# One head's order of steps rewritten on four engines of an attention kernel, with the score masks of every head written by ScalarE, and five edits ahead of the loop

## The chip, the cores and the metric

One NeuronCore of a Trainium2 chip runs the whole program in one launch. Its engines work side by side, each through its own list in order: TensorE (PE in the profile, its weight loads PEld), VectorE (DVE), ScalarE (ACT), GpSimd (POOL) and SyncE (SP), which only issues DMAs. Engines wait for each other through counting semaphores. The metric is device time in microseconds; lower is better.

## What is computed

x has 8 sequences of 128 tokens and 512 features. A LoRA-adapted linear layer makes h. Attention over h has 32 query heads, 8 key and value heads, head size 128, int4 weights with a scale per 128 inputs, rotary position and a causal mask. A LoRA pair and a feed-forward part with int8-rounded weights and activations follow.

```python
    x = x + _L0_attn_ref(_L0_cond_ref(x, itok_B_0_23, L0_cond_W, L0_cond_b, L0_cond_lora_As, L0_cond_lora_Bs), ...)
    x = x + _L0_ffn_ref(_L0_cond2_ref(x, L0_cond2_A, L0_cond2_B, itok_B_4_50), ...)
...
        q = _dequant_matmul(hidden_states, qw_q, scales_q).reshape(b, s, NH, HD).transpose(0, 2, 1, 3)
        q = _apply_rope(q, cos, sin)
        k = _apply_rope(k, cos, sin)
        scores = jnp.einsum('bhqd,bhkd->bhqk', q, k) / math.sqrt(HD)
        scores = jnp.where(causal[None, None], scores, jnp.finfo(scores.dtype).min)
        attn = jax.nn.softmax(scores.astype(jnp.float32), axis=-1).astype(q.dtype)
        ctx = jnp.einsum('bhqk,bhkd->bhqd', attn, v)
        return _dequant_matmul(ctx, qw_o, scales_o)
```

## The kernel before

**Stages.** x and W are turned, h is made in two halves (f = 0 and 1, four sequences each) and split into an upper and a lower fp16 part (h_hi, h_lo). Then comes the loop over 8 groups g (one key and value head each) with 4 query heads h in each; group 0 and group 7 are written out (`first`, `last`), groups 1 to 6 are a hardware loop. Then the second LoRA pair and the feed-forward part.

**Steps.** A step (`double_step`) is four fp16 matmuls of 128x512 into one of three PSUM pairs (pair0 to pair2, two banks each). `(Q, j)`, `(K, j)` and `(V, j)` project input block j of the next head's query or of the next group's key or value; the partial results must be scaled by block, so each step is drained on its own: block 0 by ScalarE (`drain_first`), blocks 1 to 3 by VectorE (`drain`), into raw_q, raw_k, raw_v. `(O, c)` multiplies the context by the output weights for output block c; VectorE adds it to accT (`add_output`), except block 3 of three heads in four, which ScalarE scales to part_out (`part_output`) and an accumulating DMA of POOL adds. The list PERIOD sets the order of steps, and `pair_of` which pair a step takes (its place in the list modulo 3), so a step may start when the step three places before it is drained (`free_pair`).

**One head beside the steps.** In the two banks flow0 and flow1, one for each half f, come in turn: scores (matmul of queries and keys), their row maxima (`maxima`, VectorE), the exponentials (`exps`, ScalarE), the row sums' reciprocals (`inverse`, VectorE), the multiplication by them (`normalise`: half 0 on POOL, half 1 on ScalarE), the turned probabilities (`turn_probs`, PE; kept in probsT by ScalarE, `keep_turned`), the context (`context`, PE), and its split in ctx_hi (ScalarE, `keep_upper_context`) and ctx_lo (VectorE, `split_context`). The causal mask reaches a score bank in one of two ways: PE adds it by a matmul with the identity (`scores` with masked false), or ScalarE writes it first (`seed_mask`) and the scores are accumulated onto it. Before, ScalarE does this for the heads 0 to 2 of a group and PE at head 3 (`SEEDED`).

**Other engines.** POOL does rotary position: a cosine and a sine product and a sum for each half (`q_cosine`, `q_sine`, `q_add`; for keys at heads 2 and 3). The sine product needs swap_q, raw_q with its halves of partitions exchanged, by a DMA of SP that is issued when (Q, 3) is drained. SP also loads the integer weights (`load_q`, `load_kv`, `load_output`); ScalarE makes them fp16 (`dequant`). At the end of a group PE turns the values of the next in two parts (`values_ahead`), through flow0 and flow1, and ScalarE keeps them in v_now.

**Ahead of the loop** the same is done for the first key, value and the first two queries in smaller pieces (`early_project`, `early_wide`, `early_groups`), in between the making of h. `lora_round(f, s)` adds the LoRA part to h by 32-row matmuls, in four rounds of which each waits for the one before; `linear(k)` is one output block of the dense part.

## Time and profile before

| | us |
|---|---|
| median of 3 runs | 559.31 |
| the runs | 554.47, 559.31, 561.33 |
| the profiled execution | 560.78 |
| its span, first to last instruction | 558.7 |

| engine | busy us | share |
|---|---|---|
| PE | 534.9 | 96% |
| PEld | 332.7 | 60% |
| DVE | 477.6 | 85% |
| ACT | 429.0 | 77% |
| POOL | 383.3 | 69% |

The page gives busy time by engine, the span in 40 slices, the DMA queues, the chain of work that ended last (82% of it PE, 8% DVE) and the costliest groups of instructions. A matmul's own time (0.38 us for 512 columns) overlaps the next one's, so what a matmul costs is the distance from its start to the next start. PEclk is the clock that PE was granted, 1 being 2.4 GHz and 0.5 being 1.2 GHz. In the order-of-time view a row has start, length, engine, source line and what is written from what; in square brackets stands the idle time ahead of it and what ended it. "PE flow L1702" is the context, L1694 the turned probabilities, L1567 the scores, L1564 the mask matmul, L1578 and L1579 the steps, L841 `keep_turned`, L1265 `add_output`, L1249 `drain`.

### The profile page before, as it was taken

The page shows a single profiled execution, that of the slowest core. Times are in us where ns is not written, and L with a number is a line of the kernel's source. Part 1 is how long each engine was busy: PE and PEld are TensorE (multiplying, and loading weights), DVE is VectorE, ACT ScalarE, POOL GpSimd, SP SyncE. Part 2 cuts the span into 40 slices and gives each one's busy share as a digit, 9 for nine tenths or more (in the row PEclk, how much of TensorE's full clock was granted, in tenths as well). Part 3 has the DMA queues.
Part 4 walks back from the last instruction along what each step waited for, and adds up shares of the span by engine and source line. Part 5 has one row for each costly group of instructions (what it writes and reads, how often), then busy time and mean ns, then how long its engine had stood idle before and what let it go on. Part 6 is the DMA issues. An engine that isn't in the chain of part 4 may idle for free.

```text
span 558.7 us, 10860 instructions
## 1 busy us (share of the span) xinstructions
PE 534.9 (96%) x3190; PEld 332.7 (60%) x3190; DVE 477.6 (85%) x629; ACT 429.0 (77%) x1091; POOL 383.3 (69%) x400
## 2 busy tenths in 40 slices
PE   8999979999999999999999999999999999987985
PEld 6744456666666666666666666666666666653442
DVE  4885957999899899989998999899989998876897
ACT  3574558878888888788878887888788878876795
POOL 3005485799779877987799779867986897741063
PEclk9989999999999999999999999999999999999899
DMA  8931344742673267327733672367336532410003
GB/s 295 271 74 38 82 107 133 170 95 57 170 178 88 57 177 175 79 66 177 176 69 75 176 181 61 82 177 168 70 82 169 131 79 72 96 38 1 1 20 132
DMA packets 41341, 63.47 MB, mean 114 GB/s; under 512 B 12452, under 2 KB 20804, under 8 KB 41316
## 3 DMA queue, kind: packets, MB, share of 16 engines
q1 hardware_dynamic: 35652, 46.94, 32.3%
q0 software_dynamic: 3648, 12.75, 11.3%
q10 hardware_dynamic: 2016, 3.48, 2.0%
q8 instruction: 12, 0.20, 0.1%
q14 instruction: 13, 0.11, 0.1%
HBM read 28.55 MB, written 2.10 MB: 55 GB/s over the span
## 4 chain that ended last, share of the span: by engine, by line
PE 82%; DVE 8%; ACT 4%; issue 2%; DMA 2%; POOL 1%; ACTq 0%; SPq 0%; DVEq 0%; POOLq 0%
PE pair L1578 22%; PE pair L1579 22%; PE flow L1702 11%; PE flow L1567 9%; PE flow L1694 6%; PE pair L1485 3%; PE pair L1507 1%; DVE y_max L1361 1%; DMA swap_q<-raw_q 1%; PE flow L1572 1%; DVE accT L1265 1%; ACT probs L779 1%; PE flow L1485 1%; DVE probs L1373 1%; DVE rope_c L1373 1%
## 5 line engine op out<-in xcount | busy, mean ns | idle before, releaser
L1265 DVE SCALAR_TENSOR_TENSOR accT<-pair,so_now,accT 128x1024 f32<-128x1024 f32 x103 | 130.9, 1277 | 19.8 <-PE pair L1579 16.2
L1249 DVE SCALAR_TENSOR_TENSOR raw_q<-pair,sc_now,raw_q 128x1024 f32<-128x1024 f32 x90 | 115.4, 1282 | 7.0 <-ACT raw_q L835 3.9
L572 POOL TENSOR_TENSOR rope_s<-swap_q,consts 128x512 f32<-128x512 f32 x62 | 85.4, 1378 | 30.6 <-DMA swap_q<-raw_q 30.6
L1578 PE MATMUL pair<-ctx_hi,wo 128*128 128x512 f16 x256 | 97.0, 379 | 4.2 <-issue 2.3
L1579 PE MATMUL pair<-ctx_lo,wo 128*128 128x512 f16 x256 | 97.0, 379 | 0.0
L1578 PE MATMUL pair<-h_hi,wq 128*128 128x512 f16 x240 | 91.0, 379 | 0.2 <-ACT raw_q L835 0.2
L779 ACT ACTIVATE probs<-flow,negmax 128x128 f32<-128x128 f32 x248 | 87.3, 368 | 4.9 <-DVE negmax L1217 4.9
L1579 PE MATMUL pair<-h_lo,wq 128*128 128x512 f16 x240 | 91.0, 379 | 0.0
L584 POOL TENSOR_TENSOR qT<-rope_c,rope_s 128x512 f32<-128x512 f32 x62 | 85.5, 1379 | 4.6
L572 POOL TENSOR_TENSOR rope_c<-raw_q,consts 128x512 f32<-128x512 f32 x62 | 77.6, 1274 | 10.7 <-DVE raw_q L1249 10.3
L1702 PEld LDWEIGHTS flow<-probsT,v_now 128*128 128x128 f32 x512 | 62.9, 193 | 19.2 <-ACT probsT L841 15.3
L1702 PE MATMUL flow<-probsT,v_now 128*128 128x128 f32 x512 | 72.3, 286 | 2.1 <-ACT probsT L841 2.0
L1567 PEld LDWEIGHTS flow<-kT,qT 128*128 128x128 f32 x496 | 65.1, 192 | 7.1 <-ACT flow L859 0.2
L1567 PE MATMUL flow<-kT,qT 128*128 128x128 f32 x496 | 65.4, 275 | 0.0
L864 ACT ACTIVATE ctx_hi<-flow,ctx_gain 128x512 f16<-128x512 f32 x64 | 43.9, 687 | 27.8 <-PE flow L1702 25.5
L610 POOL TENSOR_TENSOR probs<-probs,rowinv 128x512 f32<-128x512 f32 x32 | 33.3, 1040 | 37.3 <-DVE rowinv L1236 37.3
L1272 DVE SCALAR_TENSOR_TENSOR ctx_lo<-flow,ctx_gain,ctx_hi 128x512 f16<-128x512 f32 x64 | 47.5, 744 | 10.7 <-ACT ctx_hi L864 10.2
L779 ACT ACTIVATION_READ_ACCUMULATOR probs<-flow,negmax 128x1 f32 x248 | 51.6, 208 | 0.0
L841 ACT ACTIVATE probsT<-flow 128x512 f32<-128x512 f32 x64 | 38.2, 596 | 8.2 <-PE flow L1694 8.2
L1578 PEld LDWEIGHTS pair<-ctx_hi,wo 128*128 128x128 f16 x256 | 25.1, 98 | 31.2 <-issue 4.1
L835 ACT ACTIVATE raw_q<-pair,sc_now 128x1024 f32<-128x1024 f32 x30 | 33.4, 1114 | 13.2 <-PE pair L1579 11.6
L1578 PE MATMUL pair<-h_hi,wkv 128*128 128x512 f16 x112 | 42.8, 383 | 0.0
(281 smaller groups left out, 1008.5 us busy)
## 6 DMA issues: line engine op xcount, KB each, us to landing
swap_q<-raw_q SPq DMA_DIRECT2D x62, 256.0 KB, 3.7
accT<-part_out POOLq DMA_DIRECT2D x22, 512.0 KB, 4.5
wq_i<-in_L_attn_qw_q SPq DMA_DIRECT2D x8, 1024.0 KB, 5.6
wo_i<-in_L_attn_qw_o SPq DMA_DIRECT2D x32, 256.0 KB, 2.8
swap_k<-raw_k SPq DMA_DIRECT2D x14, 256.0 KB, 3.6
wkv_i<-in_L_attn_qw_k SPq DMA_DIRECT2D x8, 256.0 KB, 3.7
wkv_i<-in_L_attn_qw_v SPq DMA_DIRECT2D x8, 256.0 KB, 4.1
stage<-in_x ACTq DMA_DIRECT2D x4, 256.0 KB, 4.7
```

Of the source, the lines that this page charges most:

```text
L572: pool.tensor_tensor(per_seq(into[:, f, :]), per_seq(source[:, f, :]), on_each_seq(table), ALU.mult).then_inc(done, 1)
L584: pool.tensor_tensor(qT[:, (h + 1) % 2, half[f]], rope_c[:, f, :], rope_s[:, f, :], ALU.add).then_inc(q_roped, 1)
L779: e = act.activation(probs[:, 0, f, seq(b)], bank[:, seq(b)], ACT.Exp, bias=negmax[:, f, b:b + 1], accum_out=rowsum[:, f, b:b + 1])
L841: act.activation(probsT[:, f, :], flow[f][:, :], ACT.Copy).then_inc(probsT_kept, 1)
L864: act.activation(ctx_hi[:, h % 2, half[f]], flow[f][:, :], ACT.Copy, scale=ctx_gain[:, 0:1]).then_inc(ctx_kept, 1)
L1249: dve.scalar_tensor_tensor(out=into, in0=flat(pair[pair_of(h, (kind, j), last, first)][:, :, :]), scalar=sc_now[:, scale_slot(kind, h), j: ...
L1265: dve.scalar_tensor_tensor(out=a, in0=flat(pair[pair_of(h, (O, c), last, first)][:, :, :]), scalar=so_now[:, (h if c == 0 else h - 1) % 2, ...
L1272: dve.scalar_tensor_tensor(out=ctx_lo[:, h % 2, half[f]], in0=flow[f][:, :], scalar=ctx_gain[:, 0:1], in1=ctx_hi[:, h % 2, half[f]], op0=A ...
L1567: mm = pe.matmul(bank[:, seq(b)], qT[:, par, t], kT[:, t], start=False, stop=(b == HB - 1), skip_group_check=masked)
L1578: pe.matmul(into[:, f, :], w, upper[:, half[f]], start=True, stop=False)
L1579: mm = pe.matmul(into[:, f, :], w, lower[:, half[f]], start=False, stop=True)
L1702: mm = pe.matmul(flow[f][:, seq(b)], v_now[:, HB * f + b, :], probsT[:, f, seq(b)], start=(b == 0), stop=(b == HB - 1), skip_group_check=True)
```

## The change

**In the loop.** PE turns the probabilities of half 0 after (Q, 1), not after (Q, 2), so two steps stand between them and the first context; a step then stands between the first context and the second turning. At head 2, (V, 1) moves behind (O, 2). ScalarE writes the mask for head 3's successor too, so no mask matmul is left in the groups' heads. The values of the next group are turned as a step of its own, (VALUES, 0), through a PSUM pair, and kept by ScalarE with one instruction of 1024 elements. ScalarE's list is written anew (below). VectorE takes the reciprocals for half 0 directly behind (O, 0) of the head before, ahead of the maxima for half 1, and those for half 1 behind (Q, 1). POOL normalises half 0 at head 0 ahead of the sine product. SP swaps before it loads output weights, and at head 1 loads query, key and value weights first. Heads 0 and 1 of the last group take the new order too; its heads 2 and 3 keep the old.

**Ahead of it.** SP issues the first full swap of raw_q ahead of the four loads for the feed-forward part, and the load of the second key and value weights ahead of two half swaps. The first step (Q, 0) stands in front of turning the first values; VectorE, not ScalarE, keeps these; the first head's (K, 1) moves ahead of its second context. ScalarE makes h_hi of one block (`HI_BY_ACT`) itself. A quarter of the first chunk of `linear(4)` stands behind each LoRA round, and only the other three chunks remain behind them.

The core of the diff:

```diff
         PERIOD = [[(Q, 0), (O, 1), (Q, 1), (Q, 2), (Q, 3), (K, 0), (O, 2), (O, 3), (K, 1), (O, 0)],
                   [(Q, 0), (O, 1), (Q, 1), (Q, 2), (Q, 3), (K, 2), (O, 2), (O, 3), (K, 3), (O, 0)],
-                  [(Q, 0), (O, 1), (Q, 1), (Q, 2), (Q, 3), (V, 0), (V, 1), (O, 2), (O, 3), (V, 2), (O, 0)],
-                  [(Q, 0), (O, 1), (Q, 1), (Q, 2), (V, 3), (Q, 3), (O, 2), (O, 3), (O, 0)]]
+                  [(Q, 0), (O, 1), (Q, 1), (Q, 2), (Q, 3), (V, 0), (O, 2), (V, 1), (O, 3), (V, 2), (O, 0)],
+                  [(Q, 0), (O, 1), (Q, 1), (Q, 2), (V, 3), (Q, 3), (O, 2), (VALUES, 0), (O, 3), (O, 0)]]
         STEPS = [(h, s) for h in range(REP) for s in PERIOD[h]]
         SKIPPED = 3
         ADDED_BY_DMA = (O, 3)
...
-            return h < SEEDED and not (last and h >= 2)
+            return not (last and h >= 2)
...
+        HI_BY_ACT = C + 1
...
+            load_kv(1)
...
+                if k == HI_BY_ACT:
+                    act.activation(h_hi[:, c, half[f]], linear_bank(k), ACT.Identity, bias=bias_gained[:, c:c + 1],
+                                   scale=gain[:, 0:1]).then_inc(hi_by_act, 1)
...
+            dequant_kv(1, 0)
             act.wait_ge(outputs_in_unit, 1)
-            for f in range(2):
-                act.wait_ge(vT_done, f + 1)
-                act.activation(v_now[:, HB * f:HB * f + HB, :], per_seq(banks[4 + f]), ACT.Copy).then_inc(v_kept, 1)
...
+                    def keep_values():
+
+                        act.wait_ge(step_done, steps_by(g, h, (VALUES, 0), first, last))
+                        act.activation(v_flat, flat(pair[pair_of(h, (VALUES, 0))][:, :, :]), ACT.Copy).then_inc(act_drained, 1)
...
                     if not (first and h == 0):
                         exps(n, 0, score_bank(0, last and h == 3))
-                        if present(h, (Q, 0), first, last):
-                            drain_query()
+                    if h < 2 and not last and not (first and h == 0):
+                        dequant_kv(g + 1, h)
+                    if present(h, (Q, 0), first, last):
+                        drain_query()
                     exps(n, 1, score_bank(1, last and h == 3))
-                    if h < 2 and not last:
-                        dequant_kv(g + 1, h)
-                    if last:
+                    if last and h >= 2:
                         normalise(1)
                     keep_turned(0)
-                    if not last:
+                    if not (last and h >= 2):
                         normalise(1)
-                    if last:
+                        keep_upper_context(0)
+                        keep_turned(1)
+                    else:
                         keep_turned(1)
                         keep_upper_context(0)
-                    else:
-                        keep_upper_context(0)
-                        keep_turned(1)
-                    if first and h == 0:
-                        seed_mask(0)
                     if h == 0 and not last:
                         act.wait_ge(k_scale_set, g + 1)
                         act.wait_ge(k_roped, 2 * g + 2)
@@ -918,13 +913,15 @@
                     if h == 2 and not last:
                         act.wait_ge(v_scale_set, g + 1)
                         drain_first(V, g + 1)
+                    seed_mask(0)
                     keep_upper_context(1)
+                    output_weights()
                     if h == 3 and not last:
-                        keep_values(g + 1, 0)
-                    if not (first and h == 0):
-                        seed_mask(0)
+                        keep_values()
+                    part_output()
                     seed_mask(1)
-                    part_output()
+                    if h < REP - 1 and present(h + 1, (Q, 0), False, last) or h == REP - 1 and not last:
+                        dequant_q(g + (h + 3) // REP, (h + 3) % REP)
...
-                    inverse(0)
+                    if first and h == 0:
+                        inverse(n, 0)
+                        for f in range(2):
+                            keep_values(f)
+                        inverse(n, 1)
                     add_output(1)
-                    if not (first and h == 0):
-                        inverse(1)
                     if last and h >= 2:
+                        inverse(n, 1)
                         add_output(2)
                         add_output(3)
                     for j in range(1, C):
                         drain(*((V, 3) if h == 3 and j == 3 else (Q, j)))
-                        if first and h == 0 and j == 1:
-                            inverse(1)
+                        if j == 1 and not (last and h >= 2) and not (first and h == 0):
+                            inverse(n, 1)
                     split_context(0)
                     if h == 1:
                         drain(K, 2)
+                    if h == 3:
+                        drain(Q, 3)
+                    if not (last and h >= 2):
+                        add_output(2)
                     if h == 2:
                         drain(V, 1)
-                    if h == 3:
-                        drain(Q, 3)
                     split_context(1)
                     if not (last and h >= 2):
-                        add_output(2)
                         add_output(3)
...
+                    if not (last and h == 3):
+                        inverse(n + 1, 0)
...
+            def linear_piece(k, b):
+
+                pe.matmul(linear_bank(k)[:, seq(b)], WT[:, 0, seq(k - C)], accT[:, 0, seq(HB + b)], start=(b == 0), stop=False,
+                          skip_group_check=True)
+
             pe.wait_ge(u_kept, 1)
             for s in range(HB):
                 lora_round(0, s)
+                linear_piece(4, s)
 
...
-            linear(4)
+            for c in range(1, C):
+                linear_chunk(4, c)
...
+                    if first and h == 0:
+                        pe.wait_ge(early_added, 18)
+                        for f in range(2):
+                            turn_values(f, banks[4 + f])
+                        pe.wait_ge(lowT_kept, 2)
...
+                    project(Q, 1)
+                    turn_probs(0)
+                    project(Q, 2)
+                    project(*((V, 3) if h == 3 else (Q, 3)))
+                    context(0)
+                    project(*((K, 0), (K, 2), (V, 0), (Q, 3))[h])
+                    turn_probs(1)
+                    output(2)
                     if h == 2:
-                        project(V, 0)
                         project(V, 1)
+                    if first and h == 0:
+                        project(K, 1)
+                    context(1)
                     if h == 3:
-                        project(Q, 3)
-                    context(1)
-                    if not (last and h >= 2):
-                        output(2)
-                    values_ahead(0)
-                    if not (last and h >= 2):
-                        output(3)
+                        values_ahead()
+                    output(3)
```

The order of PE's instructions at three places. REGISTER_ALU and ISA rows are waits on a loop-dependent count.

**PE, head 0 of a group in the loop, from behind the turning of half 0 (flow0<-consts,probs) on.** Before, one step, (Q, 3) into pair1, stands in front of the context, and the turning of half 1 behind it:

```order
L1660 REGISTER_ALU
L1578 MATMUL pair1<-h_hi,wq 128x512
L1579 MATMUL pair1<-h_lo,wq 128x512
L1578 MATMUL pair1<-h_hi,wq 128x512
L1579 MATMUL pair1<-h_lo,wq 128x512
L1699 ISA
L1700 ISA
L1702 MATMUL flow0<-probsT,v_now 128x128 x4
L1694 MATMUL flow1<-consts,probs 128x128 x4
```

After, two steps, (Q, 2) into pair0 and (Q, 3) into pair1:

```order
L1596 MATMUL pair0<-h_hi,wq 128x512
L1597 MATMUL pair0<-h_lo,wq 128x512
L1596 MATMUL pair0<-h_hi,wq 128x512
L1597 MATMUL pair0<-h_lo,wq 128x512
L1675 REGISTER_ALU
L1596 MATMUL pair1<-h_hi,wq 128x512
L1597 MATMUL pair1<-h_lo,wq 128x512
L1596 MATMUL pair1<-h_hi,wq 128x512
L1597 MATMUL pair1<-h_lo,wq 128x512
L1716 REGISTER_ALU
L1717 ISA
L1719 MATMUL flow0<-probsT,v_now 128x128 x4
```

One step more now separates the turning from the context, and the turning of half 1 no longer follows the context.

**PE, head 3 of a group, behind the second context.** Before, (O, 2) has been issued, the values' first half is turned through flow0, then (O, 3), then the mask (tri_b) and the scores:

```order
L1710 REGISTER_ALU
L1572 MATMUL flow0<-consts,raw_v 128x128 x4
L1578 MATMUL pair2<-ctx_hi,wo 128x512
L1579 MATMUL pair2<-ctx_lo,wo 128x512
L1578 MATMUL pair2<-ctx_hi,wo 128x512
L1579 MATMUL pair2<-ctx_lo,wo 128x512
L1719 REGISTER_ALU
L1725 REGISTER_ALU
L1564 MATMUL flow0<-tri_b,ident_b 128x512
L1567 MATMUL flow0<-kT,qT 128x128 x4
```

After, the values are one step of eight turned blocks into pair2, and no mask matmul is left:

```order
L1719 MATMUL flow1<-probsT,v_now 128x128 x4
L1725 REGISTER_ALU
L1730 MATMUL pair2<-consts,raw_v 128x128 x8
L1675 REGISTER_ALU
L1596 MATMUL pair0<-ctx_hi,wo 128x512
L1597 MATMUL pair0<-ctx_lo,wo 128x512
L1596 MATMUL pair0<-ctx_hi,wo 128x512
L1597 MATMUL pair0<-ctx_lo,wo 128x512
L1738 ISA
L1742 REGISTER_ALU
L1743 REGISTER_ALU
L1585 MATMUL flow0<-kT,qT 128x128 x4
```

The values left the flow banks, and what was two mask matmuls on PE is now two instructions of ScalarE.

**ACT, the end of head 3 and the loop's edge.** Before (v_now<-flow keeps the values, wo and wq are weights made fp16, probs the exponentials):

```order
L864 ACTIVATE ctx_hi<-flow0,ctx_gain 128x512
L841 ACTIVATE probsT<-flow1 128x512
L864 ACTIVATE ctx_hi<-flow1,ctx_gain 128x512
L851 ISA
L852 ACTIVATE v_now<-flow0 128x512
L362 REGISTER_ALU
L362 COMPARE_AND_BRANCH
L754 ACTIVATE wo<-wo_i 128x512
L754 ACTIVATE wq<-wq_i 128x512
L852 ACTIVATE v_now<-flow1 128x512
L779 ACTIVATE probs,rowsum<-flow0,negmax 128x128 x4
```

After (flow0<-consts and flow1<-consts write the mask):

```order
L842 ACTIVATE probsT<-flow1 128x512
L860 ACTIVATE flow0<-consts 128x512
L865 ACTIVATE ctx_hi<-flow1,ctx_gain 128x512
L757 ACTIVATE wo<-wo_i 128x512
L852 REGISTER_ALU
L853 ACTIVATE v_now<-pair2 128x1024
L860 ACTIVATE flow1<-consts 128x512
L757 ACTIVATE wq<-wq_i 128x512
L361 REGISTER_ALU
L361 COMPARE_AND_BRANCH
L782 ACTIVATE probs,rowsum<-flow0,negmax 128x128 x4
```

The weights moved from a head's start to its end, and the mask of the first half now stands ahead of the second ctx_hi. The same order holds at heads 0 to 2.

## Rows read from the trace of the kernel before

**Rows 1.** The page's first line: the span of the profiled execution.

```profile
span 558.7 us, 10860 instructions
```

**Rows 2.** Busy time in stretches: from:to, length, engines, PEclk, DMA share, GB/s.

```profile
33.50:37.00 3.50, 3.50 (x12) 1.51 (x5) 3.36 (x10) 3.29 (x6) 0.43 (x3) 0.51 0.17 23
...
81.10:85.00 3.90, 3.88 (x16) 3.08 (x17) 2.30 (x3) 2.81 (x7) 3.50 (x5) 0.56 0.33 63
99.80:155.00 55.20, 55.18 (x333) 35.33 (x333) 49.84 (x57) 45.55 (x123) 45.50 (x48) 1.00 0.51 125
```

**Rows 3.** PE in the loop, in order of time: start us, us, what [idle before].

```profile
166.38 1.05 PE L1702 MATMUL flow<-probsT,v_now 128*128 128x128 f32 x8
167.27 0.38 PE L1578 MATMUL pair<-ctx_hi,wo 128*128 128x512 f16 x1
...
182.69 0.38 PE L1579 MATMUL pair<-ctx_lo,wo 128*128 128x512 f16 x1
182.97 0.39 PE L1564 MATMUL flow<-tri_b,ident_b 128*128 128x512 bf16 x1
183.19 1.05 PE L1567 MATMUL flow<-kT,qT 128*128 128x128 f32 x8
...
190.01 0.60 PE L1694 MATMUL flow<-consts,probs 128*128 128x128 f32 x4
190.45 0.38 PE L1578 MATMUL pair<-h_hi,wq 128*128 128x512 f16 x1
...
191.31 1.15 PE L1702 MATMUL flow<-probsT,v_now 128*128 128x128 f32 x8
192.46 0.66 PE L1694 MATMUL flow<-consts,probs 128*128 128x128 f32 x4
192.96 0.38 PE L1578 MATMUL pair<-h_hi,wkv 128*128 128x512 f16 x1
```

**Rows 4.** Waits, whole span: engine line <- releaser: us, times, longest.

```profile
PEld flow L1702 <- ACT probsT L841: 15.3, 48, 0.3
```

**Rows 5.** Order of time: DVE, POOL, PE at one head, ACT at another.

```profile
173.43 0.68 DVE L1217 TENSOR_REDUCE negmax<-flow 128x4 f32<-128x512 f32 x1
...
174.27 1.04 POOL L610 TENSOR_TENSOR probs<-probs,rowinv 128x512 f32<-128x512 f32 x1 [0.79 <-DVE rowinv L1236]
...
175.96 0.60 PE L1694 MATMUL flow<-consts,probs 128*128 128x128 f32 x4
...
190.65 0.60 ACT L841 ACTIVATE probsT<-flow 128x512 f32<-128x512 f32 x1
```

**Rows 6.** Groups of DVE in 99.8 to 155.0 us: busy, mean ns, idle.

```profile
L1265 DVE SCALAR_TENSOR_TENSOR accT<-pair,so_now,accT 128x1024 f32<-128x1024 f32 x14 | 17.8, 1278 | 1.8 <-PE pair L1579 1.8
L1249 DVE SCALAR_TENSOR_TENSOR raw_q<-pair,sc_now,raw_q 128x1024 f32<-128x1024 f32 x12 | 15.4, 1280 | 0.5
```

**Rows 7.** Order of time, first head of the first group: PE, SP's queue, ACT.

```profile
73.66 1.09 PE L1572 MATMUL pair<-consts,raw_v 128*128 128x128 f32 x8 [0.85 <-DVE raw_v L1210]
...
78.11 0.39 PE L1578 MATMUL pair<-h_hi,wq 128*128 128x512 f16 x1 [0.23 <-ACT raw_q L835]
...
81.12 1.85 PE L1702 MATMUL flow<-probsT,v_now 128*128 128x128 f32 x8 [1.97 <-ACT probsT L841]
...
69.89 1.11 SPq L464 DMA_DIRECT2D swap_q<-raw_q  x2
...
76.94 1.11 ACT L835 ACTIVATE raw_q<-pair,sc_now 128x1024 f32<-128x1024 f32 x1 [1.45 <-DMA swap_q<-raw_q]
```

**Rows 8.** Order of time, ahead of the loop: PE, then DVE.

```profile
31.80 0.50 PE L1498 MATMUL pair<-raw_v,qT 32*128 32x128 f32 x8 [0.17 <-PE pair L1498]
...
54.28 2.30 DVE L1148 CAST h_hi<-h_scaled 128x512 f16<-128x512 f32 x2 [2.44 <-ACT h_scaled L730]
```

**Rows 9.** Order of time, first head of the last group: PE.

```profile
468.11 0.66 PE L1694 MATMUL flow<-consts,probs 128*128 128x128 f32 x4 [0.32 <-ACT probs L846]
...
473.55 0.38 PE L1578 MATMUL pair<-ctx_hi,wo 128*128 128x512 f16 x1 [0.23 <-DVE accT L1265]
```

More of the change, by code:

```diff
@@ L264, in present @@
                 return False
-            return not (last and (s[0] in (K, V) or s[0] == Q and h >= 2))
+            return not (last and (s[0] in (K, V, VALUES) or s[0] == Q and h >= 2))
         def added_by_dma(h, s, last):
@@ L494, in body @@
                         swap(swap_k, raw_k, swapped_k)
+                    if h < 2 or not last:
+                        load_output(g + h // 2, (h + 2) % REP)
             body(0, True, False)
@@ L1704, in context, with values_ahead @@
                         mm.then_inc(pv_done, 1)
[L1706 to L1712 removed]
+                    def values_ahead():
+                        pe.wait_ge(dve_drained, drains_by(g, h, (V, 3), first, last))
+                        free_pair(VALUES, 0)
+                        into = pair[pair_of(h, (VALUES, 0))]
+                        for f in range(2):
+                            for b in range(HB):
+                                mm = pe.transpose(into[:, f, seq(b)], raw_v[:, f, seq(b)], ident)
+                        mm.then_inc(step_done, 1)
                     def scores_ahead(f):
@@ L1728, in body @@
                     project(Q, 0)
-                    output(1)
-                    project(Q, 1)
-                    project(Q, 2)
-                    if not last:
-                        turn_probs(0)
-                    project(*((V, 3) if h == 3 else (Q, 3)))
+                    if first and h == 0:
+                        pe.wait_ge(early_added, 18)
+                        for f in range(2):
+                            turn_values(f, banks[4 + f])
+                        pe.wait_ge(lowT_kept, 2)
+                    output(1)
                     if last and h >= 2:
```

106 lines of the change are left out of this document (41 added, 65 removed).

## The prediction

> **What bounds the kernel now.** The page comes first: the span is 558.7 us [rows 1], and the time of that execution, 560.78, lies 2.1 above it. I sum against 560.8; the median of the runs, 559.31, is 1.5 lower. The chain that ended last is four fifths PE, and the stretch view says where that holds: in 99.8 to 155.0 us, one group of four heads, PE is busy in 55.18 of 55.20 us at clock 1.00, VectorE in 49.84, ScalarE in 45.55, POOL in 45.50 [rows 2]. So in the loop PE alone sets the pace, and "busy" hides what it could save. The order-of-time view shows it as start-to-start distances. A step is 0.86 (190.45 to 191.31), a turning 0.44 (190.01 to 190.45). A context costs 0.89 where two steps stand ahead of it (166.38 to 167.27), but 1.15 with one step (191.31 to 192.46), and the turning behind that one takes 0.50 instead of 0.44 (192.46 to 192.96) [rows 3]. The waits name the cause: the context's weight loads waited 48 times for ScalarE's copy L841, 15.3 us [rows 4]. A mask matmul costs 0.28: it starts 0.28 behind the matmul ahead of it, of which 0.22 is that one's own length, and itself holds PE for 0.22 (182.69, 182.97, 183.19) [rows 3], so the two mask matmuls at a group's edge are 2 x (0.06 + 0.22) = 0.56.
>
> **The loop, part by part.**
> The first context. ScalarE's copy starts at 190.65 and takes 0.60 [rows 5], so it ends at 191.25 and PE starts at 191.31. With (Q, 2) moved behind the turning, PE asks 0.86 later. The copy is then 0.8 us early, and the context costs 0.89. The turning of half 1 follows a step and costs 0.44. Gain 0.26 + 0.06 = 0.32 a head. It holds for 27 heads: 32 without the first and without the last group's four. 27 x 0.32 = 8.6 us. The second context still has one step in front and I credit it nothing.
> The weight load itself may be priced another way. The Trainium skill (TensorE: Matmul & The Clock Gate, LDWEIGHTS) estimates a load of 128 columns at 128/1.2 = 107 ns. If only such a load were exposed, the term would be 27 x 0.11 = 2.9 us, and the sum 546.2. The measured distances, 1.15 against 0.89, are of the same instructions and decide.
> The masks. Seven group edges times 0.56 = 3.9 us off PE. ScalarE pays two more masks, bounded by its copies of the same 512 elements, 0.60 each [rows 5], and saves one instruction of the two that kept the values. Its load becomes about 45.55 + 1.2 = 46.8 a group.
> The values turn in one step of eight blocks instead of two of four: the same 0.88. It adds a stop: (O, 0) of head 3 takes pair2 behind it and needs ScalarE's copy.
> The new period is 55.2 - 4 x 0.32 - 0.56 = 53.4 us. Does anyone else fit no longer? VectorE has 49.84 of work in it (93%), ScalarE 46.8 (88%), POOL 45.5 (85%). VectorE's instructions are the same ones, 14 and 12 of its two largest groups, of 1.28 us [rows 6]; only the order moves. So I look at waits, not loads.
> The tightest is the turning of half 0. POOL normalises at 174.27 for 1.04, ends at 175.31, and PE turns at 175.96, spare 0.65 [rows 5]. The turning moves 0.86 forward, which would leave it 0.21 late; but VectorE now takes the reciprocal ahead of a maximum of 0.68 (173.43) [rows 5], so about 0.4 to spare is left. At head 0 POOL no longer has a sine product in front. Following each engine's new list over one head with the durations above, I find 0.2 to 0.4 us spare for the first context, the second half's mask and (O, 0) of head 3. All are positive and all are thin. I take no loss; the bounds are nothing and 0.3 a head, which is giving back the gain.
> SP: the weight loads now go ahead of head 1's swap. What they wait for (weights made at the end of head 0 and early in head 1) is done some 6 us before (Q, 3) is drained, so the swap isn't held; cost nothing.
>
> **The first head.** Before it, PE waits 0.85 for the last piece of V, 0.23 for ScalarE's drain, and 1.97 for the first context's copy [rows 7]. Then it runs at clock 0.56 for 3.9 us, which costs 3.9 x 0.44 = 1.7 [rows 2]. The reason is a queue: the swap is issued at 69.89 behind four loads, ScalarE's drain starts only at 76.94, released by it [rows 7], and everything of the head stands behind that drain. With the loads behind the swap I expect the drain near 74, where POOL's cosine products end. (Q, 0) fills the 0.85. ScalarE has no values to keep and no output weights in between. So 0.85 + 0.23 + 1.97 + 1.7 = 4.75 goes. What comes: the mask of half 0 now stands behind the key's drain, and the split of half 1 ends late for (O, 0); I put 0.5, between 0 and 1.1. Net 4.3.
>
> **Ahead of the loop.** LoRA rounds have 0.17 us of idle each [rows 8]; the quarter chunks (0.22 each) fit there, so one chunk, 0.88, goes. Right behind, PE runs at clock 0.51 for 3.5 us, costing 1.7 [rows 2]; denser rounds may or may not prevent that, and from ends equally far I take half, 0.9. For h_hi, VectorE's two casts take 2.30 us together [rows 8] on the path to the second half's projections; with one of them on ScalarE's side I count 0.65 (bounds 0 and 1.5).
>
> **The last group.** Heads 0 and 1 wait 0.32 before the second turning and 0.23 before (O, 0) [rows 9] and have no K step to space things. The new order removes some and keeps some: 0.5 a head, 1.0 in all (0 to 1.6).
>
> **Sum.** 8.6 + 3.9 + 4.3 + 0.9 + 0.9 + 0.65 + 1.0 = 20.25. 560.8 - 20.25 = 540.5 us. 2%, about what a measurement of this kernel can tell from no change, is 11.2 us, so faster begins at 548.1.
>
> **Rivals.**
> A, the forecast: 535 to 546, chance 0.70. Both ends of the clock and the first head's bounds lie in it.
> B, only a weight load's worth comes back at the first context (2.9 for 8.6): 546.2. For it: the second context with one step ahead still loses some. Against it: 0.89 at 166.38 with two steps [rows 3]. Chance 0.07.
> C, ScalarE comes late. Its list is full of waits, and the thin margins turn into 0.3 us a head at the first context or the mask. 31 x 0.3 = 9.3, so 549.8. For it: ScalarE goes from 45.55 of 55.2 to 46.8 of 53.4. Against: it idles between, and what it does late is now the weights, which nobody wants soon. Chance 0.10.
> D, the other sign: VectorE stands still at the new place of the first reciprocal. There it waits for the exponentials of the next head, and behind it are the maxima of half 1 and (O, 1)'s drain, for whose pair PE waits. Each us that the exponentials are late is then a us of PE in each of 31 heads. It decides at 20.25 / 31 = 0.65 us; at 1.0 us the time is 571. For it: VectorE has only 7% left. Against: by my walk the exponentials end at about the time (O, 0) is drained. Chance 0.06.
> E, still faster than 535: both low-clock stretches gone and the second context's wait too. Chance 0.07.
> The change not doing what it says would be B.
>
> **Numbers.** Faster: A, B, E, 0.84 in all, of which I give 0.01 to same; the chances are 0.83, 0.12, 0.05, D being partly within 2%. Range 535 to 549: all of A and B and the near part of C.
>
> **What would show it.** In the changed kernel's order-of-time view the first context's distance should be 0.89 and no mask matmul should stand at group edges; a group should take 53.4 us. PE idle ahead of the first context of all should be under 0.3, and ScalarE's first drain should start near 74 (less what was won before). Wrong would be: weight loads of the context still waiting for the copy (B, C), PE waiting for VectorE's drains or reciprocal waits growing (D), or PE waiting for the mask or ctx_lo.

## The result, and the profile after

The median is 540.57 us (538.78 to 543.61, 4 runs) against 558.54 (554.47 to 561.33, 4 runs): a ratio of 0.9698, 95% interval 0.9652 to 0.9744. Run again later with 6 runs, the changed kernel took 539.84 against 557.57, a ratio of 0.9681 (0.9648 to 0.9713). The profiled execution took 543.61, its span is 541.1.

The page of the changed kernel, its first lines:

```profile
span 541.1 us, 10845 instructions
...
PE 520.7 (96%) x3182; PEld 333.6 (62%) x3182; DVE 475.0 (88%) x630; ACT 428.6 (79%) x1097; POOL 383.6 (71%) x400
```

Its busy time in three stretches (from:to, length, PE, PEld, DVE, ACT, POOL, PEclk, DMA share, GB/s), which answer to [rows 2]: at the end of the LoRA rounds and behind them, around the first context, and one group of the loop:

```profile
33.50:37.00 3.50, 3.50 (x25) 2.08 (x26) 3.33 (x11) 2.19 (x4) 0.43 (x3) 1.00 0.15 19
76.00:80.00 4.00, 4.00 (x26) 2.64 (x25) 3.79 (x5) 3.23 (x8) 3.58 (x5) 1.00 0.00 0
183.22:236.64 53.42, 53.42 (x329) 35.54 (x328) 49.41 (x56) 45.53 (x125) 45.38 (x48) 1.00 0.52 128
```

A group takes 53.42 us instead of 55.26, TensorE is still the one that is always busy, and both low-clock stretches of [rows 2] are at full clock. One head of the loop on TensorE, in order of time, beside [rows 3] (L1719 is the context, L1709 the turning, L1596 and L1597 the steps):

```profile
236.64 1.05 PE L1719 MATMUL flow<-probsT,v_now 128*128 128x128 f32 x8
237.53 0.38 PE L1596 MATMUL pair<-h_hi,wkv 128*128 128x512 f16 x1
...
238.40 0.60 PE L1709 MATMUL flow<-consts,probs 128*128 128x128 f32 x4
238.83 0.38 PE L1596 MATMUL pair<-ctx_hi,wo 128*128 128x512 f16 x1
...
239.69 1.15 PE L1719 MATMUL flow<-probsT,v_now 128*128 128x128 f32 x8
240.68 0.38 PE L1596 MATMUL pair<-ctx_hi,wo 128*128 128x512 f16 x1
```

The first context costs 0.89 (236.64 to 237.53), the turning 0.43, the second context, with one step ahead, 0.99.

Where the time went, by marks on TensorE that both kernels have. The column "predicted" divides the prediction's own terms over the same stretches:

| from the mark ahead to | before | after | gained | predicted |
|---|---|---|---|---|
| first LoRA round | 31.13 | 31.68 | -0.55 | 0 |
| first projection | 42.21 | 41.00 | 1.76 | 1.8 |
| second scores | 71.75 | 70.53 | 0.01 | 0.65 |
| (Q, 0) of head 1, group 0 | 89.66 | 84.50 | 3.94 | 4.3 |
| (Q, 0) of head 0, group 1 | 131.30 | 124.77 | 1.37 | 1.52 |
| (Q, 0) of head 0, group 7 | 462.87 | 445.60 | 10.74 | 11.04 |
| first matmul behind the loop | 510.51 | 493.17 | 0.07 | 1.0 |

Behind that another 0.2 to 0.3 is gained, so the spans differ by 17.6. Where the programs are the same, these distances are the same within a few hundredths in all the runs below, but for four places: what comes ahead of the first LoRA round (28.8 to 31.7), one or two of the six groups (0.1 to 0.3 longer, up to 1.4 in three runs; most of it is explained behind run 7), the last group, and the feed-forward part. In this profile it is the first of the six groups, 53.69 instead of 53.42.

### The profile page after: what moved, and what is told of

Read it like the earlier page. It is cut to its first block, busy times and chain, and to the rows that moved or that the text cites. A ratio compares the mean times of both kernels' runs of the same rounds, so it can differ in the third digit from the quotient of the medians.

```text
span 541.1 us, 10845 instructions
## 1 busy us (share of the span) xinstructions
PE 520.7 (96%) x3182; PEld 333.6 (62%) x3182; DVE 475.0 (88%) x630; ACT 428.6 (79%) x1097; POOL 383.6 (71%) x400
## 4 chain that ended last, share of the span: by engine, by line
PE 82%; DVE 9%; ACT 4%; issue 2%; DMA 2%; POOL 1%; ACTq 0%; SPq 0%; DVEq 0%; POOLq 0%
PE pair L1596 22%; PE pair L1597 22%; PE flow L1719 10%; PE flow L1585 10%; PE flow L1709 5%; PE pair L1497 2%; DVE raw_q L1255 2%; PE pair L1519 2%; PE flow L1497 1%; PE pair L1730 1%; DVE y_max L1373 1%; DVE probs L1385 1%; ACT probs L782 1%; DVE rope_c L1385 1%; DMA stage<-in_x 1%
## 5 line engine op out<-in xcount | busy, mean ns | idle before, releaser
L1596 PE MATMUL pair<-ctx_hi,wo 128*128 128x512 f16 x256 | 97.0, 379 | 4.2 <-ACT wo L757 1.6
L1597 PE MATMUL pair<-ctx_lo,wo 128*128 128x512 f16 x256 | 97.0, 379 | 0.0
L1596 PE MATMUL pair<-h_hi,wq 128*128 128x512 f16 x240 | 91.0, 379 | 0.0
L1597 PE MATMUL pair<-h_lo,wq 128*128 128x512 f16 x240 | 91.0, 379 | 0.0
L1719 PEld LDWEIGHTS flow<-probsT,v_now 128*128 128x128 f32 x512 | 64.8, 191 | 13.3 <-ACT probsT L842 7.0
L1719 PE MATMUL flow<-probsT,v_now 128*128 128x128 f32 x512 | 69.5, 279 | 0.1
L782 ACT ACTIVATION_READ_ACCUMULATOR probs<-flow,negmax 128x1 f32 x248 | 53.3, 215 | 0.0
L842 ACT ACTIVATE probsT<-flow 128x512 f32<-128x512 f32 x64 | 38.9, 608 | 17.6 <-PE flow L1709 17.6
L847 ACT ACTIVATE probs<-probs,rowinv 128x128 f32<-128x128 f32 x128 | 40.9, 391 | 13.3 <-DVE rowinv L1242 12.6
L1219 DVE TENSOR_REDUCE negmax<-flow 128x4 f32<-128x512 f32 x62 | 42.0, 677 | 3.2 <-PE flow L1585 2.5
L1596 PE MATMUL pair<-h_hi,wkv 128*128 128x512 f16 x112 | 42.5, 379 | 0.0
```

The source lines that it names most:

```text
L782: e = act.activation(probs[:, 0, f, seq(b)], bank[:, seq(b)], ACT.Exp, bias=negmax[:, f, b:b + 1], accum_out=rowsum[:, f, b:b + 1])
L1219: dve.tensor_reduce(negmax[:, f, :], per_seq(score_bank(f, last_head)), AX.X, ALU.max, negate=True).then_inc(negmax_done, 1)
L1596: pe.matmul(into[:, f, :], w, upper[:, half[f]], start=True, stop=False)
L1597: mm = pe.matmul(into[:, f, :], w, lower[:, half[f]], start=False, stop=True)
L1719: mm = pe.matmul(flow[f][:, seq(b)], v_now[:, HB * f + b, :], probsT[:, f, seq(b)], start=(b == 0), stop=(b == HB - 1), skip_group_check=True)
```

## Experiments

Eleven runs are edits of the changed kernel, one is the changed kernel again. Runs 1, 3, 4 and 5 were on one chip, the others on another. The ratios are to the kernel before; to compare with, the changed kernel itself took 539.84 us (run 11), and run 5, on the first of the two chips, 539.79 with an edit that changed nothing. The intervals of the times are about as wide as most of these effects, so each reading below rests on distances in one trace. "From the first LoRA round" leaves out the part ahead that varies.

**1. The turning put back.**

```diff
                     project(Q, 1)
-                    turn_probs(0)
                     project(Q, 2)
+                    turn_probs(0)
```

> The changed kernel with one thing put back: TensorE turns the probabilities of half 0 behind (Q, 2), so only one step stands between them and the first context. Theory (the first context pays whatever part of its weight loads waits for ScalarE's copy): its distance goes from 0.89 back to 1.15, the turning of half 1 stays at 0.44, so 0.26 a head and 1.04 a group, 53.43 to 54.47; over 30 heads 7.8 us. Rival B (only a weight load of 0.11 is exposed): 0.44 a group, 53.87, 3.3 us in all. Rival D (VectorE or POOL set the pace, not TensorE): the group stays at 53.4.

Measured: 543.25 us, ratio 0.9764 (0.9727 to 0.9800). Five of the six groups took 53.86 to 53.88, one 54.06: 0.45 a group in the five, of which 0.36 are the first contexts. TensorE in it:

```profile
142.52 1.15 PE L1719 MATMUL flow<-probsT,v_now 128*128 128x128 f32 x8
143.50 0.38 PE L1596 MATMUL pair<-h_hi,wkv 128*128 128x512 f16 x1
```

With one step ahead the context costs 0.98, not 1.15. That is rival B's price, and the reading of [rows 3] on which the largest term rests was wrong: 0.26 was not what ScalarE's copy cost. (By the formula of the Trainium skill, TensorE: Matmul & The Clock Gate, LDWEIGHTS, a load of 128 columns is estimated at 107 ns. The 0.09 that the late copy exposes lies near it, but the profile gives 191 ns for a weight load of the context, so that it is one such load is not shown.) What else ended the 1.15 stood in a row that I had not read, ScalarE in the kernel before at the same head:

```profile
191.15 1.26 ACT L846 ACTIVATE probs<-probs,rowinv 128x128 f32<-128x128 f32 x4
```

It ends at 192.41, and TensorE turns half 1 at 192.46. So the turning may have waited for the normalised half, or it costs more directly behind a context.

The kernel before also had the price of a context with one step ahead and a step behind, at the same head. It is the second context:

```profile
193.82 1.15 PE L1702 MATMUL flow<-probsT,v_now 128*128 128x128 f32 x8
194.80 0.38 PE L1578 MATMUL pair<-ctx_hi,wo 128*128 128x512 f16 x1
```

That is 0.98 too. The 0.89 of [rows 3] (166.38) was a second context as well, with a step behind it, and the 1.15 a first one with the turning behind it: the two differ in what follows, not only in the steps ahead.

**2. The turning directly behind the context**, which tells these apart.

```diff
                     context(0)
-                    project(*((K, 0), (K, 2), (V, 0), (Q, 3))[h])
                     turn_probs(1)
+                    project(*((K, 0), (K, 2), (V, 0), (Q, 3))[h])
```

> The changed kernel with the turning of half 1 directly behind the first context again, the step that stood between them behind it; two steps still stand ahead of the context. What it tells apart: why the first context cost 1.15 before, of which turn_late gave back only 0.09 a head. Theory 1 (the turning waits for ScalarE's normalised probabilities, which end 1.14 behind the first context's start in the changed kernel): 1.19 to the turning and 0.50 for it, 0.36 a head, the group 53.42 to 54.87. Theory 2 (the turning's own weight loads can't go under the context's short matmuls): 1.06 and 0.50, 0.23 a head, 54.35. The prediction's step (only the number of steps ahead of the context counts): 0.06 a head, 53.67.

Measured: 547.87 us, ratio 0.9843 (0.9768 to 0.9919), a group 54.59. TensorE at one head:

```profile
237.44 1.05 PE L1719 MATMUL flow<-probsT,v_now 128*128 128x128 f32 x8
238.65 0.66 PE L1709 MATMUL flow<-consts,probs 128*128 128x128 f32 x4
239.14 0.38 PE L1596 MATMUL pair<-h_hi,wkv 128*128 128x512 f16 x1
```

1.21 and 0.49, as theory 1 has it, and ScalarE's multiplication of half 1 starts at 237.31 and takes 1.28, so it ends 0.06 ahead of the turning. Its group is 0.28 shorter than I wrote, because the step that moved now stands ahead of the second context, which costs 0.89 instead of 0.98 at three heads; 4 x 0.36 - 3 x 0.09 = 1.17, and 53.42 + 1.17 = 54.59. The turning waits for ScalarE. So the 0.32 a head are 0.09 for the copy, 0.17 for the normalised half, and 0.06 for a turning that starts from a wait. They don't come one by one: context and turning together take 1.70 in this run and took 1.65 before, so two steps ahead alone bring nothing. The step behind the context brings 0.23 (run 1 has it), and only then are the 0.09 of the copy to be had.

**3. The masks on TensorE at head 3 again** (seven pairs of mask matmuls; ScalarE doesn't write these).

```diff
-            return not (last and h >= 2)
+            return h < REP - 1 and not (last and h >= 2)
...
```

> The changed kernel with the masks of the heads that follow head 3 added by TensorE again, two mask matmuls at each of seven group edges, and ScalarE without them. Theory (TensorE sets the pace and each mask matmul costs its distance): 0.43 to 0.56 a group, 53.43 to between 53.86 and 53.99, 3.0 to 3.9 us in all. Rival C (ScalarE is late for something): the 1.04 us of ScalarE that go give part of it back, less than 0.4 a group.

Measured: 544.30 us, ratio 0.9782 (0.9752 to 0.9811), a group 53.86. That is 2 x 0.22, the matmuls alone. The 0.13 that is missing to my 0.56 was there in the kernel before, where a mask started 0.28 behind its neighbour, but doesn't come back with the mask. Which of the edits at the group's edge took it away, no run shows. Nothing of it is given back by ScalarE.

**4. The LoRA rounds side by side again.**

```diff
                 lora_round(0, s)
-                linear_piece(4, s)
...
-            for c in range(1, C):
-                linear_chunk(4, c)
+            linear(4)
```

> The changed kernel with the four LoRA rounds next to each other again and the whole first chunk of linear(4) behind them. From the changed kernel's trace, where the stretch from the first round to the first projection took 9.32 us against 11.08 before: if the clock falls to half again behind the rounds, 1.76 us come back and the filled idle time was worth nothing (theory: what the spacing brought was the clock, and the pieces cost as much as they filled). The prediction's own step says 0.88 for the chunk, with the clock apart: 0.9 if the clock stays, 2.6 if it falls. If the clock's fall had another cause, and the pieces cost what they fill: 0.

Measured: 541.70 us, ratio 0.9730 (0.9697 to 0.9762). From the first LoRA round to the first projection 11.06 us, against 9.32: 1.74. A stretch behind the rounds in this run, then TensorE's rows of it, then those of the changed kernel:

```profile
33.00:34.00 1.00, 1.00 (x9) 0.51 (x3) 1.00 (x1) 0.64 (x1) 0.43 (x3) 0.50 0.32 33
```

```profile
32.65 0.65 PE L1510 MATMUL pair<-raw_v,qT 32*128 32x128 f32 x8 [0.17 <-PE pair L1510]
33.23 8.64 PE L1497 MATMUL pair<-accT,WT 128*128 128x512 f32 x16
```

```profile
34.23 0.50 PE L1510 MATMUL pair<-raw_v,qT 32*128 32x128 f32 x8
34.67 0.49 PE L1556 MATMUL pair<-accT,WT 128*128 128x128 f32 x2
34.99 6.17 PE L1497 MATMUL pair<-accT,WT 128*128 128x512 f32 x14
```

The clock falls to 0.50 for some 3.5 us again, half of which is the 1.74. The filled idle time brought nothing: a round alone took 0.67 with its 0.17 of idle [rows 8], a round and a piece take 0.85 (0.44 from 34.23 to 34.67 are the round's). So a piece has TensorE for 0.42 (the last, with the long chunks behind it, for 0.32), not for the 0.22 of its columns. From the first round to the linear part it is 3.31 (31.68 to 34.99) against 2.43 (31.13 to 33.56) before, 0.88 more, exactly the chunk that went. Further on this run loses more than the 1.74: its first context is 2.29 later (47.07 from the first LoRA round, against 44.78), since other waits come up, one of 0.63 for ScalarE ahead of the second scores. How these hang on the 1.74 was not followed.

**5. Four loads ahead of the swap, and 6. all six.** In the first the four loads of the feed-forward part stand ahead of the first full swap again; in the second `load_kv(1)` too, SyncE's order of before.

```diff
+            load_kv(1)
+            for m, row in enumerate((gamma, beta, b1)):
+                sp.dma_start(rows[:, m, :], row.partition_broadcast(P)).then_inc(d_rows, 16)
+            sp.dma_start(b3_col[:, :], b3.rearrange("(c p) -> p c", p=P)).then_inc(d_rows, 16)
             sp.wait_ge(early_sin, 4)
             sp.wait_ge(early_added, 15)
             swap(swap_q, raw_q, swapped_q)
```

> The changed kernel with SyncE's four loads for the feed-forward part ahead of the first full swap again. Theory (the swap behind these loads held ScalarE's first drain): the drain, now at 73.3, starts near 75.7 (76.9 before, less 1.2 won ahead of it); the first context comes 2.0 to 2.4 later, TensorE idles there, and if the clock falls in the narrow stretch another 1.6 goes: 2.0 to 4.0 us in all. Rival (the drain waits for POOL's cosine products, not for the swap): less than 0.3.

> The changed kernel with all six loads (second key and value weights, the four of the feed-forward part) between the last half swap and the first full swap, SyncE's order of before. With only the four of them there nothing was lost, since the swap waited for POOL's sine product anyway. Theory (the transfer of the swap is slow behind the transfers of the six loads: 7.0 us from issue to ScalarE's drain before, 4.5 to 4.6 in the changed kernel and with four loads): 7 us again, the drain and the first context 2.2 to 2.4 later, and up to 1.7 more if TensorE's clock falls there; 2.2 to 4.0 us on the first context, counted from the first LoRA round (44.8 us in the changed kernel). Rival (the drain's place in ScalarE's own list, not the transfer, was what mattered): less than 0.3.

Measured with four: 539.79 us, ratio 0.9701 (0.9664 to 0.9738), first context 44.79 us from the first LoRA round against 44.78. My expectation fell. SyncE and POOL in that run:

```profile
64.88 0.43 SPq L473 DMA_DIRECT2D b_col<-in_L_ffn_b  x1
...
66.03 1.28 POOL L531 TENSOR_TENSOR rope_s<-swap_q,consts 128x512 f32<-128x512 f32 x1
```

The loads are issued long before POOL's sine product ends at 67.31, for which the swap must wait, and the swap goes out at 67.34. In the kernel before it was the same: the sine product ended at 69.85, the swap was issued at 69.89 [rows 7]. It never stood in a queue.

Measured with six: 542.44 us, ratio 0.9746 (0.9691 to 0.9800). The swap is issued at the same place (66.20, 36.99 us from the first LoRA round in both), but ScalarE starts 7.35 us later instead of 4.62:

```profile
73.55 1.11 ACT L836 ACTIVATE raw_q<-pair,sc_now 128x1024 f32<-128x1024 f32 x1 [4.39 <-DMA swap_q<-raw_q]
...
74.72 0.39 PE L1596 MATMUL pair<-h_hi,wq 128*128 128x512 f16 x1 [1.43 <-ACT raw_q L836]
76.69 1.61 PE L1719 MATMUL flow<-probsT,v_now 128*128 128x128 f32 x8 [0.94 <-ACT probsT L842]
```

Its stretch behind that:

```profile
78.00:80.00 2.00, 2.00 (x7) 0.91 (x7) 1.90 (x2) 0.69 (x1) 1.00 (x3) 0.50 0.00 0
```

The first context is 2.70 later, TensorE idles 2.37 and its clock falls to 0.50 behind that; at head 1 4.1 us are lost, all that the first head had gained. What held the drain was the transfer, slow while the data of six loads issued just ahead of it still moved. Whether it is their number, their shape or their time was not tried: with six the last load was issued 1.3 us ahead of the swap, with four 2.5.

**7. The values turned first and kept by ScalarE**, with SyncE's new order.

> The changed kernel with the first values turned ahead of (Q, 0) and kept by ScalarE again, SyncE's new order left as it is. Theory, from the changed kernel's trace: TensorE waits 0.95 for the values before it turns them, and ScalarE's two copies stand ahead of its drain; the first context comes 0.9 to 1.3 later (44.8 to between 45.7 and 46.1, counted from the first LoRA round). Rival (since putting the six loads back alone cost 4.1 us at head 1, which is the whole gain of the first head, these two edits bring nothing): less than 0.3.

Measured: 541.75 us, ratio 0.9711 (0.9660 to 0.9762); the first context 46.09 against 44.8, so 1.3 us. These edits are worth 1.3 once the swap is fast, and the two parts overlap: 4.1 and 1.3 are more than the 3.94 gained.

This trace also has something that I overlooked, and that the edit has nothing to do with. The first of the six groups takes 54.83 instead of 53.42. ScalarE in it, then TensorE:

```profile
148.22 1.11 ACT L879 ACTIVATE part_out<-pair,so_now 128x1024 f32<-128x1024 f32 x1 [1.64 <-DMA accT<-part_out]
...
149.96 1.15 PE L1586 MATMUL flow<-kT,qT 128*128 128x128 f32 x8 [1.14 <-ACT flow L863]
```

ScalarE must wait for the accumulating DMA before it writes part_out anew, and since the change the mask of half 1 stands behind that instruction. When the transfer is late, TensorE waits for the mask. The same wait is 0.51 in the first profile of the changed kernel (its group is 0.27 longer), 0.89 in those of runs 2 and 3 (0.65 longer), 0.24 in run 4's (nothing), and the kernel before has none. That is of rival C's kind, at one or two heads of an execution.

**8. h_hi of the one block by VectorE again.**

> The changed kernel with h_hi of that one block made by VectorE again. The prediction's step says 0.65 us (0 to 1.5) on the path to the projections of the second half. From the changed kernel's trace: the second half's projections came 0.44 us nearer, but a projection of the first half waited 0.25 for VectorE and lay 0.5 later. Theory (the edit does nothing measurable in sum): within 0.3 us at the second scores, counted from the first LoRA round (38.85 us in the changed kernel). The prediction's step: 0.65 more, 39.5.

Measured: 539.66 us, ratio 0.9674 (0.9623 to 0.9725). The second scores lie 38.90 us from the first LoRA round, against 38.85: 0.05. The edit does nothing.

**9. The reciprocal behind the maxima again, and 10. one more instruction on ScalarE.**

```diff
-                    if not (last and h == 3):
-                        inverse(n + 1, 0)
                     if not (last and h >= 2):
                         maxima(n + 1, 1)
+                    if not (last and h == 3):
+                        inverse(n + 1, 0)
```

```diff
                     part_output()
+                    wait(act, extra_done, n)
+                    act.activation(per_seq(probs[:, 1, 0, :]), on_each_seq(tri), ACT.Copy).then_inc(extra_done, 1)
                     seed_mask(1)
```

> The changed kernel with VectorE's reciprocal for half 0 behind the maxima of half 1 again. Theory (it stands in front because the turning of half 0 has only 0.38 us to spare, 0.17 at head 3): the reciprocal comes 0.60 later, POOL's product with it, TensorE waits about 0.2 at each turning, 0.6 to 0.9 a group, 53.42 to between 54.0 and 54.3, 5 us in all. Rival D of the prediction (standing at the reciprocal costs VectorE, and TensorE with it): the group gets shorter than 53.4, by up to 0.4, which VectorE waits there at head 3.

> The changed kernel with one more instruction of 512 elements on ScalarE in every head, ahead of the mask of half 1; it writes a place that nobody reads. It takes 0.52 from its neighbours. Theory (spare from the changed kernel's trace: the mask ends 0.41, 0.39, 0.58 and 0.69 ahead of the scores at heads 0 to 3): heads 0 and 1 lose 0.11 and 0.13, the others nothing, the group 53.42 to about 53.7. Rival C of the prediction (ScalarE is at its end once the masks are its): 0.3 to 0.52 a head, 54.6 to 55.5.

Measured, reciprocal: 547.39 us, ratio 0.9835 (0.9773 to 0.9896), a group 54.50, 1.07 more. Its waits, from 180 to 450 us:

```profile
PEld flow L1709 <- POOL probs L610: 10.8, 20, 0.6
```

In the changed kernel this row reads 1.3 us in 6 times, the longest 0.2. A delay of 0.60 costs 0.27 a head, more than the 0.6 to 0.9 a group that I had expected, so the spare is about 0.33; rival D's mechanism isn't there, on the contrary.

Measured, ScalarE: 545.94 us, ratio 0.9809 (0.9737 to 0.9877), a group 54.18, 0.76 more or 0.19 a head for 0.52 put in, again a spare of 0.33. TensorE now waits ahead of the scores of half 1 at every head, where I had expected it at two:

```profile
PEld flow L1588 <- issue: 8.3, 20, 0.6
```

The row names no releaser; at the head where I looked the mask ended at 189.18 and the scores started at 189.31. Neither my 0.25 a group nor rival C's 1.2 to 2.1 came. ScalarE isn't at its end, but a third of a microsecond is all it has.

**11. The changed kernel again, and 12. a version with both ends reordered.** In the last group VectorE takes (O, 3) of head 2 behind the splits and maxima, and TensorE head 3's (O, 3) behind the contexts. In the first head the split of the first context and its mask go ahead.

```diff
                         context(0)
                         context(1)
+                        if h == 3:
+                            output(3)
...
                     if last and h == 2:
                         maxima(n + 1, 1, True)
+                        add_output(3)
+                        inverse(n + 1, 0)
```

> The changed kernel itself, unchanged, as the one to which the other three of this chip are held. A group of 53.4 us again, 9.3 us from the first LoRA round to the first projection, 44.8 to the first context. Theory (what comes ahead of the first LoRA round and in the last group varies from execution to execution by about 1 us each, as the eight traces so far do): the span between 537 and 542.

> A version meant to be better than the changed kernel, with the same work. In the last group VectorE no longer stands at (O, 3) of head 2, which waits 2.2 to 3.4 us for the accumulating DMA, with the context's splits and the maxima of the last head queued behind it: it comes behind them; the reciprocals of the last head go ahead of its output blocks, and TensorE does that head's (O, 3) behind the contexts, where it idles 1.6. In the first head VectorE splits the first context ahead of the last query drain, and ScalarE writes the mask ahead of the key's drain. Theory: the last group, from its first context to the first LoRA matmul behind the loop, 41.7 to 42.8 in the traces so far, gets 1 to 2 us shorter; the first head 0.35. Together 1.3 to 2.4 us, 0.2 to 0.4%, at the edge of what the times can tell. Rival (VectorE's four last additions of 1.2 set the end whatever stands ahead of them): less than 0.4.

Measured: 539.84 and 539.57 us, ratios 0.9681 (0.9648 to 0.9713) and 0.9679 (0.9646 to 0.9713): no difference that a time can show. The spans are 537.7 and 537.4. In the last group and behind it 0.5 was gained, and in the first head 0.8 at the first scores, 0.35 at the second, and nothing by the first context of group 1. The time came back as other waits of TensorE, here of the new version in the last group and at the first head:

```profile
479.71 0.39 PE L1606 MATMUL pair<-ctx_hi,wo 128*128 128x512 f16 x1 [1.11 <-DVE accT L1274]
...
81.19 0.38 PE L1606 MATMUL pair<-ctx_hi,wo 128*128 128x512 f16 x1 [0.82 <-ACT wo L757]
```

The first was 0.57 in the changed kernel, the second 0.28. My 1.3 to 2.4 did not come; the 0.3 between the spans is within the rival's 0.4, and VectorE works without a gap from 486.6 to 492.8 in this version, on additions.

The repeat of the changed kernel explains part of the first profile. VectorE at (O, 3) of the last group's head 2, in the first profile and in the repeat:

```profile
477.39 1.28 DVE L1271 SCALAR_TENSOR_TENSOR accT<-pair,so_now,accT 128x1024 f32<-128x1024 f32 x1 [3.35 <-DMA accT<-part_out]
```

```profile
474.82 1.28 DVE L1271 SCALAR_TENSOR_TENSOR accT<-pair,so_now,accT 128x1024 f32<-128x1024 f32 x1 [2.21 <-DMA accT<-part_out]
```

The accumulating transfer came 1.1 us later in the first, and the last group took 42.82 us from its first context instead of 41.69.

## Why the prediction was right, and where it was not

The forecast was 540.5 and the median is 540.57. That is closer than the steps deserve, and luck: the sum gave 20.25 us, the two profiled executions differ by 17.2 and the medians by 18.0. The profiled execution from which I subtracted was 2.2 us above its median (558.54), and this cancels the 2.3 that the sum has too much.

- **The loop** (8.6 + 3.9) came: 12.11 of 12.5 in the two rows of the table, 53.42 us a group against 53.4 predicted. The size stood on distances that exist in the trace on both sides (1.15, 0.89, 0.50, 0.44), so it didn't need the right cause. The cause was wrong in its larger part. "The copy is then 0.8 us early, and the context costs 0.89" is true, but the late copy had cost 0.09 (run 1), and 0.17 went to ScalarE's normalised half (run 2). The step that failed is the comparison of 0.89 with 1.15 in [rows 3], which took a second context for a first. The edit removes both, because a step now stands between the context and the turning as well. Rival B had the right price for the copy. Without the moved K step, not even that would have come at the first context: run 2 is that kernel, and its context and turning take 1.70 against 1.65 before.
- **The masks**: 0.44 for the matmuls (run 3); the rest of 0.56 went too, but not with the masks, and no run shows with what.
- **The margins**, "0.2 to 0.4 us spare" and "all are thin": held. Measured from outside they are 0.33 for the reciprocal and 0.33 for ScalarE (runs 9 and 10). C didn't come but for the late transfer behind run 7, 0.27 us in this profile. D didn't come, and its sign was wrong: without the early reciprocal the loop loses 1.07 a group.
- **The first head** (4.3, came 3.94): the waits that went are as described, and 0.55 for the mask and 0.28 ahead of (O, 0) came, 0.83 where I had put 0.5. The two signs held: TensorE has no wait ahead of the first context, and the drain starts at 73.29. The step "The reason is a queue" failed. The swap was issued the moment POOL allowed it; its transfer was slow behind six loads (runs 5 and 6). And the two causes overlap (run 7), where I took them as terms.
- **LoRA rounds** (0.9 for the chunk, 0.9 as half a chance for the clock): came as 1.76, all of it the clock and nothing from the filled idle time (run 4), since a piece costs 0.42 and not 0.22. Two wrong sizes with a right sum, which is luck.
- **h_hi** (0.65): 0.05. The two casts were on VectorE's path, but making one of them elsewhere moved TensorE by no more than that (run 8).
- **The last group** (1.0): 0.07 in this profile. In the repeat it is 46.44 us against 47.64, so 1.2. But VectorE's wait for the accumulating transfer was 3.35 here, 2.21 in the repeat and 2.87 in the kernel before, and the 1.14 between the first two is the 1.13 between their groups. At an equal wait both give an estimated 0.5 for the new order, half of what I had put.

## What to carry to other kernels

A distance between starts on the busy engine prices an edit well, but not its cause: before naming one, read what the next instruction waits for too, and let one run move the neighbour. Where a DMA comes late, look at when it was issued and when it could have been; if these agree, it did not stand in a queue, and the transfers that still move are the next suspect. Filling idle time on an engine brings nothing by itself if the filler needs more than the hole, but it can hold the clock. Once the engines beside the busy one have a third of a microsecond to spare a head, an instruction that waits for a DMA must not stand ahead of one that the busy engine needs. And an end where one engine works without a gap gains little from another order (run 12).

## What the runs showed of the hardware

- A swap of 2 x 256 KB needed 4.5 to 4.6 us from issue to its reader with nothing or four earlier loads ahead, and 7.0 to 7.4 behind six loads, the last issued 1.0 to 1.3 us before.
- TensorE's clock fell to 0.50 for about 3.5 us behind four 32-row rounds with 0.17 us of idle each, and in both kernels that idled 2.4 to 3 us around the first context (before, and with six loads); with 0.42 us of 128-row matmuls in each hole it stayed at 1.00. In run 3's profile, and in no other, it also fell ahead of the first LoRA round, for about 3.4 us. In the feed-forward part it fell in the first profiles of both kernels and in none of the twelve later ones, which made 0.9 us between two executions of the same program (43.17 and 42.28 us from behind the loop to the end).
- An fp32 piece of 128 columns costs TensorE 0.42 us between two rounds (0.32 ahead of a long chunk) where a chunk of 512 costs 0.86: about half the price for a quarter of the columns.
- An accumulating DMA of 512 KB was waited for 2.2 us in one execution and 3.35 in another of the same kernel, at the same place; in the loop ScalarE waited for one between 0.24 and 1.64 us, at one or two heads of an execution, in most traces of the changed kernel and its edits.
